# The first sequence's output projection and its first chunk's norm, moved from behind attention into attention's last two blocks

## The reference

```python
def _adaln(x, c, ...):
    norm = jnp.maximum(jnp.linalg.norm(x, axis=-1, keepdims=True) * x.shape[-1] ** (-0.5), EPS)
    return x / norm * norm_w * scale[:, None, :] + shift[:, None, :]

x = x + _attention(_adaln(x, c, ...), attention_mask, qkv_w, proj_w, proj_b)   # 16 heads of 16, softmax over 1024 keys
x = x + _mlp(_adaln(x, c, ...), mlp_w1, mlp_b1, mlp_w2, mlp_b2)
# _mlp: h = x @ w1.T + b1; x1, x2 = split(h); silu(x1) * x2 @ w2.T + b2, inner width 1024
```

## Time and profile before

| | us |
|---|---|
| median of 3 runs | 3241.91 (3240.42 to 3242.19) |
| the profiled execution | 3239.28 |
| its span, first to last instruction | 3237.5 |
| start of END's first matmul | 3047.65 |
| TensorE busy in the span | 3178.2 (98%) |
| VectorE, ScalarE, GpSimd busy | 2845.2, 2803.9, 2340.3 |

### The profile page before, as it was taken

How to read it: one execution, slowest core, us unless ns; L and a number is a source line. 1 busy time by engine, 2 the same in 40 slices (tenths; PEclk the granted TensorE clock), 3 DMA queues, 4 the chain that set the end, 5 groups by cost and what they waited for, 6 DMA issues and landing times.

```text
span 3237.5 us, 59446 instructions
## 1 busy us (share of the span) xinstructions
PE 3178.2 (98%) x22634; PEld 2504.1 (77%) x22634; DVE 2845.2 (88%) x2848; ACT 2803.9 (87%) x4611; POOL 2340.3 (72%) x1128
## 2 busy tenths in 40 slices
PE   8999999999999999999999999999999999999899
PEld 5899998999999998999998999899888542222244
DVE  3999999999999999999999999999999578888121
ACT  6999999999999999999999999999999336777620
POOL 1999999999999999999999999998999220000000
PEclk8999999999999999999999999999999999999999
DMA  4332222222222222222222222221212043322000
GB/s 139 103 91 84 69 73 70 73 68 73 70 73 90 74 68 79 67 74 68 75 74 69 71 68 73 70 75 66 86 66 71 33 98 66 72 33 33 13 7 20
DMA packets 212559, 222.00 MB, mean 69 GB/s; under 512 B 86545, under 2 KB 162321, under 8 KB 212017
## 3 DMA queue, kind: packets, MB, share of 16 engines
q1 hardware_dynamic: 212274, 218.20, 23.4%
HBM read 197.43 MB, written 18.21 MB: 67 GB/s over the span
## 4 chain that ended last, share of the span: by engine, by line
PE 80%; ACT 9%; DVE 5%; POOL 3%; issue 3%; DMA 0%; DVEq 0%; ACTq 0%; SPq 0%
PE psum L1702 22%; PE psum L1470 18%; PE psum L1696 16%; PE psum L1693 12%; PE psum L1779 4%; ACT arena L1132 4%; PE psum L1768 3%; POOL arena L825 3%; PE psum L1753 3%; ACT arena L1114 3%; DVE arena L1360 3%; DVE row_max L1423 1%; PE psum L1722 1%; ACT arena L1157 1%; ACT arena L961 0%
## 5 line engine op out<-in xcount | busy, mean ns | idle before, releaser
L1360 DVE TENSOR_TENSOR_SCAN arena<-arena,psum 128x512 f32<-128x512 f32 x2048 | 2370.8, 1231 | 51.6 <-PE psum L1696 39.7
L825 POOL TENSOR_TENSOR arena<-arena 128x1024 f32<-128x1024 f32 x1024 | 2219.4, 2182 | 214.8 <-DVE arena L1360 190.7
L1132 ACT ACTIVATE arena<-arena,a_neg 128x512 f32<-128x512 f32 x2048 | 1498.0, 763 | 32.4 <-PE psum L1696 31.9
L1702 PE MATMUL psum<-ident,arena 128*128 128x128 f32 x8192 | 1228.1, 273 | 1.7 <-POOL arena L825 1.7
L1114 ACT ACTIVATE arena<-arena,bT 128x512 f32<-128x512 f32 x1536 | 1171.7, 763 | 0.0
L1696 PE MATMUL psum<-ident,arena 128*128 128x128 f32 x6144 | 1006.8, 273 | 0.0
L1702 PEld LDWEIGHTS psum<-ident,arena 128*128 128x128 f32 x8192 | 959.2, 141 | 2.1 <-POOL arena L825 2.1
L1693 PE MATMUL psum<-arena 128*128 128x128 f32 x4096 | 816.9, 281 | 12.6 <-ACT arena L1114 9.3
L1693 PEld LDWEIGHTS psum<-arena 128*128 128x128 f32 x4096 | 646.4, 191 | 222.8 <-issue 148.9
L1696 PEld LDWEIGHTS psum<-ident,arena 128*128 128x128 f32 x6144 | 741.8, 142 | 0.0
L1470 PE MATMUL psum<-arena 128*128 128x512 f32 (+1 forms) x1440 | 671.0, 587 | 8.5 <-DVE arena L1232 2.9
(11 more groups left out here) (120 smaller groups left out, 858.9 us busy)
## 6 DMA issues: line engine op xcount, KB each, us to landing
arena<-bc_dram SPq DMA_DIRECT2D x256, 512.0 KB, 3.6
arena<-diag_dram SPq DMA_DIRECT2D x248, 128.0 KB, 2.1
arena<-qk_dram SPq DMA_DIRECT2D x96, 128.0 KB
diag_dram<-arena SPq DMA_DIRECT2D x32, 256.0 KB, 4.3
qk_dram<-arena SPq DMA_DIRECT2D x8, 768.0 KB, 3.5
arena<-in_x SPq DMA_DIRECT2D x4, 512.0 KB, 11.0
arena<-skip_w SPq DMA_DIRECT2D x64, 32.0 KB, 2.0
arena<-sums_dram SPq DMA_DIRECT2D x64, 32.0 KB, 1.8
```

Source lines behind the costliest of these rows:

```text
L825: pool.tensor_tensor(out[:, :, way], h_now[:, :, way], c_row, ALU.mult)\
L1132: act.activation(decay[:, w % AHEAD, f], dt_[:, u % 2, f], ACT.Exp, scale=a_neg[:, d, f, st:st + 1])\
L1360: dve.tensor_tensor_scan(hs[:, w % RING, f, rows][:, way], decay[:, w % AHEAD, f, way], psum[:, 4 + n % U_BANKS, way], end_state(w - DS, f ...
L1702: return pe.matmul(psum[:, c, f * P:(f + 1) * P], hs[:, w % RING, f, at:at + P], ident[:, :], is_transpose=True, start=False, stop=w % DS ...
```

## The change

Two projections (chunks 0 and 1) and `square`, `sum` and `std` of chunk 0's norm leave END and become a list TAIL. On TensorE its ten matmuls are put one by one into ten steps of blocks 14 and 15 (TAIL_AT), between the second and third score matmul where the step is even, behind the weighing where it is odd. On VectorE the two additions, a square (before, ScalarE's) and the floor stand in block 15's part of its program, ahead of and behind the reciprocal of block 14. On ScalarE Ln and Exp stand behind step 13 of block 15. The first diff places are memory, the order END and the place list; the later ones are ScalarE's, VectorE's and TensorE's programs. Chunk 0's `scale` stays in END, now as its first step, and END's other steps are put in a new order. The square's and the norm's buffers get other places in memory.

```diff
+STD_STEP = 13
-        NORM_AT = {"ln0": (24064, 19968), "ln1": (26112, 22016), "rms0": (26624, 28672), "rms1": (26624, 28672)}
+        NORM_AT = {"ln0": (24064, 19968), "ln1": (26112, 22016), "rms0": (26624, 28672), "rms1": (26624, R_AW)}
+            if (name, i) == ("rms1", 0):
+                at = R_PARTS
-        END = [("proj", 0)] + steps("square", "rms1", 0) + [("proj", 1)] + steps("sum std scale", "rms1", 0) + steps("square", "rms1", 1)\
-            + [("proj", 2)] + steps("sum std scale", "rms1", 1)\
-            + up("rms1", 0, 0, 8) + [("proj", 3)] + steps("square sum std scale", "rms1", 2) + up("rms1", 0, 8, 12)\
-            + steps("square sum std scale", "rms1", 3) + up("rms1", 0, 12, N1)
+        TAIL = [("proj", 0)] + steps("square", "rms1", 0) + [("proj", 1)] + steps("sum std", "rms1", 0)
+        TAIL_AT = [(BLOCKS - 2, m) for m in (1, 4, 7, 10, 13)] + [(BLOCKS - 1, m) for m in (0, 3, 6, 8, 10)]
+        END = steps("scale", "rms1", 0) + steps("square", "rms1", 1) + up("rms1", 0, 0, 4) + steps("sum std scale", "rms1", 1)\
+            + up("rms1", 0, 4, 8) + [("proj", 2)] + steps("square", "rms1", 2) + up("rms1", 0, 8, 10) + [("proj", 3)]\
+            + steps("sum std scale", "rms1", 2) + steps("square", "rms1", 3) + up("rms1", 0, 10, 12)\
+            + steps("sum std scale", "rms1", 3) + up("rms1", 0, 12, N1)
+        place_tiles(TAIL, lambda g: 5 + g % 3)
...
+            act.preload_act_table_set(EXP_LN)
+                    if (v, m) == (BLOCKS - 1, STD_STEP):
+                        std("rms1", 0)
             copy_attn(BLOCKS - 1)
-            act.preload_act_table_set(EXP_LN)
             do(END)
...
+            def square_first():
+
+                dve.wait_ge(s["x_updated"], NEED["rms1", 0])
+                dve.tensor_tensor(sq("rms1", 0), x[:, :, 0, tok(0)], x[:, :, 0, tok(0)], ALU.mult).then_inc(s["squared"], 1)
...
+                    if (v, m) == (BLOCKS - 1, 0):
+                        add_attention(0)
+                        square_first()
+                    if (v, m) == (BLOCKS - 1, RECIP_STEP):
+                        add_attention(1)
+                        floor("rms1", 0)
             reciprocal(BLOCKS - 1)
+            dve.wait_ge(s["s2_full"], 2 * BLOCKS * BLOCK)
             do(END)
...
+            tail = (piece for step in TAIL for piece in tile(*step))
...
+                    if (v, m) in TAIL_AT:
+                        if (v, m) == TAIL_AT[0]:
+                            pe.wait_ge(s["scores_free"], ALL_SCORES)
+                            pe.wait_ge(s["top_copied"], B * HG)
+                        next(tail, None)
...
+            for _ in tail:
+                pass
             weigh_v(BLOCKS - 1, QT - 1)
```

More of the change, by code:

```diff
@@ L36 @@
 BLOCK = 2 * QT
+BLOCKS = B * HG * HALVES
 UNITS = 2 * B * HALVES
@@ L476, in side_tile @@
             side.append((kind, i))
-        BLOCKS = B * HG * HALVES
         ALL_SCORES = B * HG * SCORE_TILES
```

## The result

The changed kernel takes 3249.17 us (median of 10, 3246.13 to 3250.35) against 3242.48 us of the kernel before (median of 10, 3240.29 to 3244.77): a ratio of 1.0019, 95% interval 1.0011 to 1.0027, or +6.7 us. The profiled execution took 3246.13 us with a span of 3244.3, against 3239.28 and 3237.5.

What follows compares the result with a forecast made beforehand. A loop between TensorE and ScalarE, neither full, bounds the blocks; TensorE alone bounds END. -8.56 + 5.8 + 0.8 + 6.1 + 0.1 + 2.4 = +6.6 us gives 3248.5, range 3244.5 to 3251.5.

Steps and rivals of the forecast that it cites:

- the line: The 0.2%, 6.5 us, that a measurement of this kernel tells from no change; the forecast sits on it.
- Removed: END on TensorE: two projections and one norm sum leave, ten matmuls of 0.856 us, -8.56 us.
- The ten in the blocks: Blocks 14 and 15: four matmuls behind a weighing cost 0.856 each, six between scores 0.37; with switching 5.8 us.
- Ln and Exp: ScalarE, step 13 of block 15: the last period's first exponential comes 0.8 us late, bounds 0 and 1.2.
- The new wait: END's head: TensorE waits for chunk 0's scale, queued on VectorE behind block 15's reciprocal: +6.1 us.
- END's order: END's new order of steps leaves TensorE holes of 0.1 us, bounds 0 and 1.
- The clock: Behind the idle at END's head TensorE runs at half clock, losing 2.4 us, bounds 0 and 3.3.
- Rival 1: The clock holds, or the half clock ends with the idle: +4.2 us, 3246.1; chance 0.1.
- rival 2: The ten matmuls hide in the blocks, their 5.8 near 0: total +0.8, 3242.7; chance 0.1.
- rival 3: No wait at END's head, VectorE gets its sums early: +0.4, 3242.3; chance 0.05, 0.03 for gains beyond.
- rival 4: Worse: holes in END's new order, or clock slow for 6.6 us: 2 and 0.9 more, 3249 to 3251.5; chance 0.15.

Runs made afterwards that it cites:

- the filled run: The changed kernel with six matmuls of 512 columns, results unread, in TensorE's wait at END's head: 3247.05 us, ratio 1.0012.
- the last version: Changed kernel with scaling ahead of block 15's reciprocal, ten matmuls at even steps, TensorE's wait for the last copy behind three up tiles: 3236.97 us, ratio 0.9983.
- odd and even extra ones: Kernel before with ten extra unread matmuls, behind the weighing at odd steps or between scores at even steps, blocks 14 and 15: odd 3252.85 us, even 3245.95.

## Why the prediction was right

It said 3248.5, +6.6 us, of which half would lie above the line; 3249.17 and +6.7 were measured. By its terms:

- **Removed, -8.56.** Not disputed by anything: twenty records of 0.43 less in END.
- **The ten in the blocks, 5.8.** Four cost 0.95 (a period of 3.41 for 2.46) and six 0.37, together 6.02, and the stretch says 6.03 (6.69 less the 0.66 below). The mechanism held to 0.01 us for the six. The term was short by what a full matmul costs more behind the 32-column weighing, which I had put at 0.05 each, between 0 and 0.15; it is 0.10 (0.96 from it to the next score, 3026.54 to 3027.50 in the changed kernel, less the 0.86 of a matmul). Whether this is a price of the change of form is not shown. Its weight load is not ahead of it: it starts with the matmul, at 3017.84, where between scores it starts 0.22 earlier (3021.48 for 3021.70). And the kernel before pays 0.10 with no change of form, at 3087.41 in END, where a full matmul behind full matmuls had been held by ScalarE's square and its load also starts with it (3087.40): from there to the next product, four records on, it is 1.82 us instead of 1.72. The Trainium skill, TensorEngine Tiling (Array Packing), Key Properties, says that changing the tiling mode drains TensorE; the 0.10 does not speak against it and does not show it.
- **Ln and Exp, 0.8.** It is 0.66: the hold before the last fourth score rose from 0.32 to 0.98. The Ln starts at 3050.28, while the record of the exponentials before it runs to 3050.42. Records of ScalarE overlap too, so its idle per period was more than the 0.39 that the prediction took off.
- **The new wait, 6.1.** It is 6.24: the reciprocal 3.60 after the copy as forecast, the scaling 2.37 with the step to it, but 0.32 instead of 0.07 from the scaling's end to the first matmul. In the filled run, where TensorE had just been at work, it was 0.06 (3064.01 to 3064.07), and in the last version 0.21. The first weight load does not explain it: it is itself recorded only at 3061.59, 0.29 behind the scaling's end. The cause stays open.
- **END's order, +0.1.** END lost 7.21, that is 8.58 less the 1.65 of half clock, and 0.28 more: the small holes of the order before have gone rather than grown. They sum to 0.27: its last norm's sum, at 3087.41, stands 0.17 behind the end of streaming and costs the 0.10 above. ScalarE's tight place behaved as worked out: table load at 3094.01, Silu 1.30 later, no drain, and Silu of up tile 12 out by 3100.77, about 2 us ahead of the bank's next use (30.8 behind the end of chunk 1's sum, 3071.95). So the drain that the Trainium skill (ScalarE: Activation LUTs, What ACT_TABLE_LOAD costs) adds to a switch of tables does not show here, and the 2.0 us that would have hung on it did not come.
- **The clock, 2.4, between 0 and 3.3.** The profiled execution lost 1.65, with matmuls at half clock from 3061.62 to 3064.99 or so, and that of the run with Ln and Exp behind the copy 2.05. The filled run is 2.1 us under in the medians of ten and eleven runs, 0.18 of it by the earlier start, as the traces have it. All are inside the range and below the 2.4.

The 2.4 was too high by a case that did not belong in it. Of the three idles that it averages, the one of 1.98 ahead of 2679.53 did not bring the half clock. The kernel before, columns as in the earlier trace rows:

```profile
2672.00:2674.00 2.00, 1.64 (x4) 0.36 (x4) 2.00 (x5) 0.00 (x0) 0.00 (x0) 0.61 1.07 131
```

The granted clock was 1.00 in the 2 us ahead of this window and fell inside it, over 3 us before that idle began at 2677.55, while TensorE worked with gaps of 0.21. The other two cases alone give 2.0.

The sum came out better than its terms. Over the traced executions they are -8.58 + 6.03 + 0.66 + 6.24 - 0.28 + 1.65 = +5.72; against the forecast's +6.6 the clock is 0.75 less, END's order 0.4 less, the blocks 0.2 more. That the medians agree with it to 0.1 is in part luck; that every term had the right sign, place and rough size, END's order of 0.1 apart, is not. The forecast's own span was also written too wide at its low end: by the clock's 1.8 and no switching cost it would begin at +5.8, not +5.3.

Rival 1 (no half clock) fell with the windows, rival 2 (hidden matmuls) with the odd and even extra ones, rival 3 (no wait) was wrong for this kernel and was then made true by one exchange on VectorE, and came out at 3240.68 where 3242.3 had been worked out for a partial one. Of rival 4 neither half came.

## What to carry to other kernels

When work is pulled forward, ask of each engine what the first step left behind it will wait for: here 8.56 us of TensorE's work were taken away, and the step that moved to the front had its input behind another engine's wait for a transfer. When two engines hold each other in a loop, neither being full, look for the one place in the period where an engine is held, since extra work there costs only what exceeds the hold (0.37 us for 0.86), while behind the weighing it cost all of it (0.95). And look at what an idle of some microseconds on TensorE does to the clock, which here made the wait a quarter to a third dearer (1.65 and 2.05 on 6.2 us).

## What the runs showed of the hardware

After the same idle of 6.96 us the matmuls ran at half clock for 3.4 us in one execution and 4.1 in another, the changed kernel's and that of the run with Ln and Exp behind the copy. The clock also fell where no such idle stood: in the kernel before it went to half between 2672 and 2674 us, where TensorE worked with gaps of 0.21 us, and was full again at 2686.10. A full fp32 matmul of 512 columns takes 0.86 us among equals and 0.96 where its weight load starts only with it, behind a weighing or behind a wait. The first matmul behind a wait started 0.05 to 0.32 us after the end of the instruction that it waited for (0.05 behind an idle of 0.72, 0.32 behind one of 6.96); what sets this is not shown.
